# Three of thirteen head sums of a graph attention's score pass go from VectorE to GpSimd

## The reference, cut to what matters

```python
Q = relu(x @ query_kernel + query_bias)[row]
K = relu(x @ key_kernel + key_bias)[col]
Qh = Q.reshape(-1, HEADS, ATT_UNITS // HEADS)      # 8 heads of 16
Kh = K.reshape(-1, HEADS, ATT_UNITS // HEADS)
att = sum(Qh * Kh, axis=-1)                         # one number an edge and head
alpha = segment_softmax(att, row, num_nodes)
```

## Time and profile before

| what | value |
| --- | --- |
| median of 3 runs | 11548.42 us (11541.08 to 11550.59) |
| the profiled execution, time | 11562.99 us |
| its span in the profile | 11561.4 us |
| VectorE busy over the span | 8515.2 us, 74% |
| GpSimd busy over the span | 1655.6 us, 14% |
| TensorE busy over the span | 8920.2 us, 77% |
| score pass, window to window | 22.05 us, 49 windows |

### The profile page before, as it was taken

One profiled execution on the slowest core, in us unless ns is written; L12 is line 12 of the kernel. 1 busy time (PEld: TensorE's weight loads), 2 busy tenths in 40 slices (PEclk: granted clock), 3 DMA queues, 4 the chain that ended last, 5 costly groups with the idle time before them and its releaser, 6 DMA issues. The chain is left out here.

```text
span 11561.4 us, 331562 instructions
## 1 busy us (share of the span) xinstructions
PE 8920.2 (77%) x101102; PEld 7210.5 (62%) x101103; DVE 8515.2 (74%) x17511; ACT 4614.1 (40%) x9076; POOL 1655.6 (14%) x2115
## 2 busy tenths in 40 slices
PE   6144557885888755899994888798899959849996
PEld 5132224664777644899993655433899946649995
DVE  7497777777999866666666666666788867788887
ACT  0021001112666411566663333476677746613332
POOL 0010000110000000466661000000000003301110
PEclk9999999998999855999997999899999979979996
DMA  1100000000444311333333999677455510000000
GB/s 37 13 0 11 4 4 8 11 11 12 168 165 165 124 36 31 112 123 125 125 123 103 320 313 322 229 250 237 131 144 144 144 40 5 5 3 3 3 3 12
DMA packets 617056, 1103.62 MB, mean 95 GB/s; under 512 B 119640, under 2 KB 207539, under 8 KB 616992
## 3 DMA queue, kind: packets, MB, share of 16 engines
q1 hardware_dynamic: 487488, 923.21, 25.3%
q10 hardware_dynamic: 121152, 168.86, 3.9%
q0 software_dynamic: 8352, 10.85, 0.4%
HBM read 901.57 MB, written 201.10 MB: 95 GB/s over the span
## 5 line engine op out<-in xcount | busy, mean ns | idle before, releaser
L2439 POOL TENSOR_TENSOR acc<-acc,m_sum 128x544 f32<-128x544 f32 (+1 forms) x637 | 816.2, 1281 | 1237.5 <-ACT m_sum L2406 953.6
L2369 PE MATMUL m_sps<-m_msg,m_oh 128*128 128x136 f32 x5096 | 722.5, 286 | 0.0
L2304 DVE TENSOR_TENSOR m_msg<-m_vps,m_msg 128x512 f32<-128x512 f32 x637 | 440.7, 692 | 361.4 <-PE m_vps L2345 269.9
L2558 DVE BATCH_NORM_STATS2 stats<-t_es 128x512 f32 x637 | 442.2, 694 | 353.0 <-ACT t_es L2591 351.6
L2759 PE MATMUL u_sps<-u_r,u_oh 128*128 128x128 f32 x5096 | 678.1, 276 | 28.7 <-ACT u_r L2717 28.7
L2570 PE MATMUL t_eps<-t_oht,p_parts 128*128 128x512 bf16 x1911 | 527.9, 386 | 211.8 <-DVE t_oht L1472 208.3
L2743 PE MATMUL u_zps<-fcs,u_a 128*128 128x128 f32 x5112 | 677.5, 276 | 7.3 <-ACT u_a L2711 7.3
L2644 PE MATMUL g_z<-g_a,fcT 128*128 128x512 f32 x1274 | 616.2, 616 | 66.2 <-ACT g_a L2633 54.4
L1408 PE MATMUL sp_out_x<-x,sp_adj_x 128*128 128x128 f32 x4802 | 661.8, 281 | 0.0
L1392 PE MATMUL sp_aps_x<-sp_ohw_x,sp_oh_x 128*128 128x128 bf16 x7644 | 545.2, 219 | 146.6 <-DVE sp_ohw_x L1359 146.6
L1421 ACT COPY sp_adj_x<-sp_aps_x 128x512 f32<-128x512 f32 x637 | 373.4, 586 | 702.4 <-PE sp_aps_x L1392 702.4
(11 more groups left out here) (584 smaller groups left out, 21493.9 us busy)
## 6 DMA issues: line engine op xcount, KB each, us to landing
u_e<-e_tiles SPq DMA_DIRECT2D x640, 256.0 KB, 2.8
e_tiles<-t_es ACTq DMA_DIRECT2D x637, 256.0 KB, 5.6
g_e<-e_tiles SPq DMA_DIRECT2D x637, 256.0 KB, 3.5
s_rows<-bucket_rows SPq DMA_DIRECT2D x148, 768.0 KB, 4.0
m_rows<-bucket_rows SPq DMA_DIRECT2D x148, 768.0 KB, 4.1
t_rows<-bucket_rows SPq DMA_DIRECT2D x148, 768.0 KB, 7.1
s_rows<-bucket_rows SPq DMA_DIRECT2D x49, 1024.0 KB, 5.3
m_rows<-bucket_rows SPq DMA_DIRECT2D x49, 1024.0 KB, 5.3
```

Of the source, the lines that this page charges most:

```text
L2369: last = nc.tensor.matmul(sps[x][:, at:at + M], oh[x][:, j * P:(j + 1) * P], msg[x][:, j * M:(j + 1) * M], start=True, stop=True)
L2439: nc.gpsimd.tensor_tensor(at, at, sums[x][:, 0:n * M], ALU.add).then_inc(added, 1)
```

## The change

GpSimd takes over the head sums of sets 2, 6 and 9. It has no single instruction here for adding along the free axis; it adds halves: the first 8 of each head's 16 elements to the last 8 (256 results), then 4 and 4 (128), 2 and 2 (64), and 1 and 1 (32 results, straight into `s_att`). Each addition waits for the one before. The last one counts `summed`. VectorE skips its reduction for these three sets. There are three new tiles `s_fold8`, `s_fold4`, `s_fold2` and one new semaphore.

```diff
@@ phase_scores
         shared = range(3, NQ - 1, 2)
+        by_pool = (2, 6, 9)
+        fold, folded = [sb(f"s_fold{n}", n * G * H) for n in (8, 4, 2)], sem("s_folded")
@@ gpsimd, in the loop over windows
                     last.then_inc(over_set, 1)
+                    half = (w & 1) * (NT * H)
+                    for i, q in enumerate(by_pool):
+                        x = X.slot(q)
+                        pool.wait_ge(prod_made[x], X.before(w, q) + 2)
+                        pool.sem_inc(rows_go, 1)
+                        left, n = prod[x][:, :].rearrange("p (m d) -> p m d", d=HD), HD // 2
+                        for f, sums in enumerate(fold):
+                            there = sums[:, :].rearrange("p (m d) -> p m d", d=n)
+                            nc.gpsimd.tensor_tensor(there, left[:, :, 0:n], left[:, :, n:2 * n], ALU.add).then_inc(folded, 1)
+                            pool.wait_ge(folded, w * (3 * len(by_pool)) + (3 * i + f + 1))
+                            left, n = there, n // 2
+                        nc.gpsimd.tensor_tensor(att[:, bass.ds(half, NT * H)].rearrange("p (j q h) -> p q j h", j=G, h=H)[:, q],
+                                                left[:, :, 0].rearrange("p (j h) -> p j h", h=H), left[:, :, 1].rearrange("p (j h) -> p j h", h=H),
+                                                ALU.add).then_inc(summed[x], 1)
@@ vector, in the loop over sets
                             hots(w + 1, q + 2 - NQ)
+                        if q in by_pool:
+                            continue
                         dve.wait_ge(prod_made[x], X.before(w, q) + 2)
                         nc.vector.tensor_reduce(att[:, bass.ds(half, NT * H)].rearrange("p (j q h) -> p q j h", j=G, h=H)[:, q],
```

## The result

The changed kernel takes 11521.3 us (median of 13 runs) against 11544.6 us for the kernel before (13 runs too, of which one took 20653.9 us and is left out of the ratio), a ratio of 0.9981 with a 95% interval of 0.9972 to 0.9990: 0.2% faster. The forecast was 11630 us, with six chances in a hundred for a gain. The score pass, where the whole change is, kept its length to within a microsecond.

| pass (tile) | before | before, again | after | after, again |
| --- | --- | --- | --- | --- |
| score (`s_prod`) | 1080.1 | 1080.0 | 1079.2 | 1079.3 |
| message (`m_sps`) | 1428.2 | 1433.7 | 1413.2 | 1413.9 |
| edge tiles (`t_eps`) | 1047.9 | 1032.9 | 1042.6 | 1046.6 |
| fully connected (`g_z`) | 676.2 | 675.6 | 664.7 | 670.4 |
| edge output (`u_zps`) | 1183.0 | 1183.0 | 1182.4 | 1182.2 |

The account below looks back on a forecast made before the run. VectorE's queue was taken to bound the score pass at 22.05 us a window; 0.26 + 0 + 1.40 = 1.66 us over 49 windows, +81, made 11548.4 into 11629, say 11630 us, range 11575 to 11745.

Parts of the forecast that it names:

- six chances in a hundred for a gain: Whole kernel: faster was given 0.06, slower 0.85, the same 0.09.
- What bounds the pass: Score pass: VectorE's queue sets it; dropped reductions give back 0.19, 0.60 and 0.19 us, about 1.0 us a window.
- GpSimd's additions: Score pass, sets 2, 6 and 9: four additions of 256, 128, 64, 32 results take 0.73, 0.46, 0.32, 0.25 us.
- Rival (a): GpSimd's additions are dearer by their short runs: +1.5 us a window, 155 us in all, 11704 us; chance 0.24.
- The joints between them: Gaps around GpSimd's additions: 0.30 us from product to first addition, then 0.18, 0.18 and 0.27; whole chain 3.47 us.
- +0.26 and 0 at sets 2 and 6: Score pass: prod(4) comes 0.26 us later after prod(2), prod(8) no later after prod(6), waiting for GpSimd's sums.
- Rival (c): Faster: each GpSimd chain fits into VectorE's remaining work, -49 us, 11500 us, if the turn is hidden too; chance 0.06.
- The collisions: Score pass: a GpSimd addition and VectorE's hots exclude each other for a whole instruction, first come first served.
- The turn of the loop: Score pass's window end: GpSimd's register loads and key copy follow set 9's last addition, delaying the next prod(0) by 1.40 us.
- +1.66 us a window: Score pass sum: 0.26 at set 2, 0 at set 6, 1.40 at the turn; 49 windows, +81 us.
- All other passes keep their times: Passes outside the score pass, the message pass among them: no change in time.

Follow-up runs that it names:

- before, again: The kernel before, unchanged, run and profiled a second time; ratio 1.0005 (0.9994 to 1.0015).
- after, again: The changed kernel, unchanged, run and profiled a second time; ratio 0.9986 (0.9977 to 0.9994) to the kernel before.
- experiment 3: The changed kernel without GpSimd's twelve additions, the sums of sets 2, 6 and 9 left out; 11509.6 us, ratio 0.9970, window 21.23 us.
- experiment 8: The changed kernel with sets 2, 4 and 7 on GpSimd in place of 2, 6 and 9; 11526.5 us, ratio 0.9986, window 21.99 us.
- experiment 7: The changed kernel with the next window's four register loads moved ahead of set 9's additions; 11505.0 us, ratio 0.9971, window 21.38 us.
- experiment 4: The kernel before with three more semaphore instructions on GpSimd ahead of the message pass's fourth addition; 11524.1 us, ratio 0.9982.
- experiment 5: The kernel before with 32 semaphore instructions on GpSimd behind the score pass's loop, executed once; 11525.2 us, ratio 0.9986.
- experiment 6: The kernel before with 16 semaphore instructions on GpSimd behind the score pass's loop, executed once; 11544.9 us, ratio 0.9999.
- experiment 2: The kernel before with only the change's three new tiles and new semaphore, unused; 11547.7 us, ratio 1.0004.
- experiment 10: The changed kernel with the edit of experiment 7 and the three semaphore instructions of experiment 4; 11501.4 us, ratio 0.9957.
- experiment 11: As experiment 10, with sets 0, 3, 6 and 9 on GpSimd in place of 2, 6 and 9; 11462.7 us, ratio 0.9924.

## Why the prediction was wrong

**What bounds the pass: nearly right.** A dropped reduction gives back what TensorE leaves: forecast 0.19 + 0.60 + 0.19 = 0.98 us a window, measured 0.18 + 0.46 + 0.17, 0.82 with the rounding (experiment 3). What was missing is at set 6, where the forecast saw nothing of TensorE: prod(7) waits for its key products (0.58 us in the row above), and starts 1.65 us after prod(6) and not 1.53.

**GpSimd's additions: right.** 0.73, 0.46, 0.32 and 0.25 us were forecast, 0.77, 0.46, 0.31 and 0.24 measured, runs of 2 to 8 elements and steps included. Rival (a) has nothing behind it. I tried no single-instruction sum on GpSimd, and no run shows that it has none.

**The joints between them: the step that failed first.** From prod(2)'s end to the first addition there are 3402.11 - 3401.94 = 0.17 us, not 0.30; from the first addition to the second and from there to the third 0.08, not 0.18 each. I had taken the gaps from additions whose queue also counts a semaphore in between the earlier trace rows. So the chain is 3.14 us where it binds (experiment 8), and not 3.47, and this mattered: against distances of 3.49 and 3.59 it leaves 0.35 to 0.45 us, where I found none. (Rival (c) has a chain of 3.14 too, but by cheaper additions, which did not come; that is chance.) The forecast +0.26 and 0 at sets 2 and 6 came out as -0.18 and -0.36.

**The collisions: right in kind, wrong in size, and wrong in order.** I had the first addition of set 2 held back until the hots were over, from 1.08 to 1.81 us behind prod(2); it starts at 0.85 and is done at 1.64, stretched by 0.07 (0.79 against 0.72 in the mean of set 9). I had the second addition of set 9 held for 0.46 us by hots(12). With shorter joints that addition starts at 0.81 us after the first (3414.08), ahead of the hots (3414.29), and it is the hots that are held, for 0.04 us. At set 6 the hots of set 9 start 0.01 us ahead of the third addition, and lose: they take 0.45 us, where the same ones take 0.35 in experiment 3, and the next product comes later by that much. The hots in the changed kernel and in experiment 3, each between prod(7) and prod(8):

```profile
3409.87 0.45 DVE L1980 TENSOR_SCALAR s_oht<-s_rows,iota_p 128x512 bf16<-128x512 bf16 x1
```
```profile
3411.19 0.35 DVE L1972 TENSOR_SCALAR s_oht<-s_rows,iota_p 128x512 bf16<-128x512 bf16 x1
```

Additions of 0.3 to 0.8 us leave little to wait for. The two places together are the 0.15 us a window that experiment 7 lacks against experiment 3; in the changed kernel the second is hidden behind the late turn. The forecast had 0.28 us for collisions at set 2 (3.75 against the chain's 3.47), 0.12 at set 6 and 0.46 at set 9.

**The turn of the loop: mechanism and its own size right, its starting point wrong.** From the last addition's start to the key copy there are 3418.20 - 3415.15 = 3.05 us, as forecast. But the last addition starts 3415.15 - 3412.42 = 2.73 us after prod(9), not 3.58; of these 0.85 us, 0.46 are the collision's and 0.39 the joints'. So from prod(9) to prod(0) the window loses 0.55 us, not 1.40. Experiment 7 shows that it is the turn: without it 0.67 us come back, which are the 0.55 and what the dropped reduction of set 9 gives.

With these the +1.66 us a window, +81 in all, become -0.18 - 0.36 + 0.55 = 0.01.

**What was not in the sum at all: the message pass.** "All other passes keep their times" is the step that failed for the sign: with every term above put right, the sum would have said no change. The gain of 23 us is about 0.49 us for most of 48 windows, decided by 0.1 us in a race between two engines. I had this collision in front of me and used it only for its price. It did not occur to me that adding instructions to one queue shifts where its later loops stand. Experiments 4, 5 and 6 show this cause by itself, without any of the change's work; experiment 2 excludes tiles and semaphores.

What stays open is why passing one place of GpSimd's program costs 0.08 us. The place behaves as a fixed boundary would: by the count of the queue's records it moves with the length of the program ahead of it, to the instruction, in the kernel before and experiments 2, 5 and 7. But no run shows what happens there.

## What to carry to other kernels

Work taken off the engine that bounds a loop is worth only what the next engine leaves, and what the receiving queue had been doing ahead of time unseen comes into the path: here four register loads, hidden in 20 us of idle time until work was put in front of them. Before choosing which pieces to hand over, compare the receiver's whole chain (3.14 us) with the room at each place, since sets 2, 6 and 9 gave nothing and sets 0, 3, 6 and 9, with the turn out of the way, 1.1 us a window. And when an engine's program changes length, look in all later loops where that engine and another contend within 0.1 us: a small gain or loss may be made there. Three idle instructions decided the race in every window of the three kernels that had them (experiments 4, 10 and 11).

## What the runs showed of the hardware that I had not expected

Hots of 1024 columns on VectorE that start 0.01 to 0.03 us before a GpSimd addition still lose to it; from 0.05 us on they win. Held-up hots are done 0.29 us after the addition's end (4840.81 + 1.64 against 4840.83 + 1.33). An addition held up by hots takes longer by what the hots have left at its start, less some 0.15 us: 0.22 where they have 0.37 left (1.56 for 1.34), 0.07 where they have 0.22 (the first addition of set 2).

GpSimd passes one addition to the next that waits for it in 0.08 us where nothing but the wait stands in the queue, 0.18 to 0.26 where an address is computed.

In several profiles, the kernel before's second one among them, the granted clock is recorded as half for the first 2880 us, and TensorE's work takes the same time. The stretch from 1100 to 1800 us in the first and the second profile of the kernel before:

```profile
1100.00:1800.00 700.00, 415.68 (x1576) 164.59 (x1576) 509.26 (x1203) 15.79 (x42) 0.00 (x0) 1.00 0.01 4
```
```profile
1100.00:1800.00 700.00, 415.81 (x1576) 165.66 (x1576) 509.27 (x1203) 15.79 (x42) 0.00 (x0) 0.50 0.01 4
```

A clock column of 1.00 or 0.50 (2.4 or 1.2 GHz) beside equal busy times and an equal pass (821.8 and 821.9 us) says that here, where TensorE is busy for 59% of the time, the column alone proves nothing of the work's speed.
